# A macaron layer on eight sequences: feed-forward blocks swapped, k projected inside the recurrence, gram products ahead of v, first block unbroken ahead of the mixture, all FIR behind it

## The reference, cut to what matters

```
x = x + 0.5 * ffn(layernorm(x))            # ffn: 256 -> 1024, gelu, 1024 -> 256
x = x + attn(layernorm(x))
x = x + 0.5 * ffn(layernorm(x))            # the same weights

def attn(x):                               # 4 heads of 64
    q, k, v = silu(short_conv(x @ Wq)), ... Wk, ... Wv          # causal, 4 taps
    beta = sigmoid(x @ Wb)                                      # one number a token and head
    delta = delta_rule(l2norm(q), l2norm(k), v * beta, k * beta) # chunks of 32: triangular inverse,
                                                                 # then a recurrence over chunks
    branches = [fir(v, 3 taps), fir(v, 31 taps), delta, v]
    w = softmax(gate(x, mean/rms/max of each branch, branches) / temp), floored, normalised
    o = rmsnorm(sum of w * branch)
    return o @ Wo
```

## Time and profile before

| | us |
|---|---|
| runs | 1223.7, 1226.2, median 1224.95 |
| the profiled execution | 1227.37 |
| its span in the trace | 1225.7 |
| TensorE busy | 1056.4 (86%) |
| VectorE busy | 820.9 (67%) |
| ScalarE busy | 549.3 (45%) |
| GpSimd busy | 415.6 (34%) |
| start of y1 (L883) of the seven passes with a back half and of the tail | 144.32, 287.65, 422.66, 558.97, 694.00, 833.65, 969.01, 1100.62 |

### The profile page before, as it was taken

How to read it: one execution, slowest core, us unless ns; L and a number is a source line. 1 busy time by engine, 2 the same in 40 slices (tenths; PEclk the granted TensorE clock), 3 DMA queues, 4 the chain that set the end, 5 groups by cost and what they waited for, 6 DMA issues and landing times.

```text
span 1225.7 us, 25639 instructions
## 1 busy us (share of the span) xinstructions
PE 1056.4 (86%) x10348; PEld 784.7 (64%) x10348; DVE 820.9 (67%) x1556; ACT 549.3 (45%) x965; POOL 415.6 (34%) x648
## 2 busy tenths in 40 slices
PE   3778598899988999899988996999988998887838
PEld 2654485378745886488736884478736885477427
DVE  5774267785687767875788666875787667863263
ACT  1154236443374337543475336453475337532322
POOL 7106500671019500681028400681028400870000
PEclk9889699899999999989999999999999999995668
DMA  5040104110040203111040203011040204020000
GB/s 153 1 102 21 34 1 97 25 31 22 18 104 1 53 1 94 28 26 27 19 104 1 52 19 86 18 24 30 18 104 1 52 1 96 9 52 1 1 0 18
DMA packets 82293, 47.45 MB, mean 39 GB/s; under 512 B 57856, under 2 KB 75776, under 8 KB 82176
## 3 DMA queue, kind: packets, MB, share of 16 engines
q1 hardware_dynamic: 82176, 45.82, 16.4%
HBM read 31.12 MB, written 14.68 MB: 37 GB/s over the span
## 4 chain that ended last, share of the span: by engine, by line
PE 57%; DVE 22%; ACT 8%; issue 5%; SPq 3%; POOL 3%; DMA 1%; DVEq 0%; ACTq 0%; POOLq 0%
PE psum L782 12%; PE psum L784 10%; PE psum L783 10%; DVE conv_acc L1363 4%; PE psum L813 4%; DVE arena L1594 3%; PE psum L975 3%; PE psum L960 3%; PE psum L994 2%; PE psum L999 2%; SPq L347 2%; PE psum L1152 2%; ACT arena L582 2%; DVE arena L1596 2%; POOL arena L522 1%
## 5 line engine op out<-in xcount | busy, mean ns | idle before, releaser
L518 POOL TENSOR_TENSOR l_prod<-arena 64x30 f32<-64x30 f32 (+14 forms) x240 | 150.8, 628 | 599.2 <-DMA arena<-l_dram 581.0
L578 ACT ACTIVATE h_f<-psum,b_col 128x512 f32<-128x512 f32 x128 | 88.0, 688 | 216.4 <-PE psum L784 206.4
L522 POOL TENSOR_TENSOR arena<-arena,l_prod 64x30 f32<-64x30 f32 (+14 forms) x240 | 157.3, 655 | 18.8
L782 PE MATMUL psum<-w_hi,h_hi 128*128 128x256 f32 x512 | 152.0, 297 | 9.2 <-DVE h_lo L1343 9.2
L784 PE MATMUL psum<-w_hi,h_lo 128*128 128x256 f32 x512 | 145.2, 284 | 0.0
L783 PE MATMUL psum<-w_lo,h_hi 128*128 128x256 f32 x512 | 145.1, 283 | 0.0
L1081 PE MATMUL psum<-v_shift,fir_w 128*32 128x512 f32 x1152 | 133.6, 604 | 3.6 <-DMA v_shift<-v_dram 3.6
L1363 DVE SCALAR_TENSOR_TENSOR conv_acc<-psum,conv_col,conv_acc 128x511 f32<-128x511 f32 x144 | 107.8, 748 | 33.5 <-ACT conv_acc L603 22.4
L782 PE MATMUL psum<-xt_hi,w_hi 128*128 128x512 f32 x256 | 109.4, 427 | 14.3 <-DVE b_half L1456 7.0
L1342 DVE CAST h_hi<-h_f 128x512 fp32r<-128x512 f32 x128 | 65.3, 510 | 76.6 <-ACT h_f L578 40.1
L782 PEld LDWEIGHTS psum<-w_hi,h_hi 128*128 128x128 f32 x512 | 98.1, 192 | 15.3 <-DVE h_lo L1343 11.1
(11 more groups left out here) (232 smaller groups left out, 2205.6 us busy)
## 6 DMA issues: line engine op xcount, KB each, us to landing
x_in<-in_L_attn_x SPq DMA_DIRECT2D x8, 512.0 KB, 4.0
v_dram<-v_fm SPq DMA_DIRECT2D x8, 512.0 KB, 2.8
v_shift<-v_dram SPq DMA_DIRECT2D x8, 512.0 KB, 5.0
out<-x_tok SPq DMA_DIRECT2D x8, 512.0 KB, 2.9
v_shift<-v_dram SPq DMA_DIRECT2D x8, 511.0 KB, 7.0
v_shift<-v_dram SPq DMA_DIRECT2D x8, 510.0 KB, 9.1
v_shift<-v_dram SPq DMA_DIRECT2D x8, 509.0 KB, 11.6
arena<-in_L_ffn_w SPq DMA_DIRECT2D x2, 1024.0 KB, 7.1
```

What stands on the lines that cost most here:

```text
L518: pool.tensor_tensor(prod, l_inv[:, k + 1:, k:k + 1].broadcast_to(shape), l_inv[:, k:k + 1, 0:k].broadcast_to(shape), ALU.mult).then_inc(i ...
L522: pool.tensor_tensor(l_inv[:, k + 1:, 0:k], l_inv[:, k + 1:, 0:k], prod, ALU.add).then_inc(inverted, 1)
L578: act.activation(h_f[:, m % 2, :], bank, ACT.Gelu, bias=b1_col[:, m:m + 1]).then_inc(read, 1)
L782: pe.matmul(dst, a_hi, b_hi, start=first, stop=False, **kw)
```

## The change

- The blocks change places. The filler of the merge and the recurrence is now the **second** block of sequence i - 1 (`upr`, `outr`); the **first** block of sequence j + 1 (`upw`, `outw`) stands as one piece behind `hidden` and ahead of the FIR. The program is now head, "zero" (a body without filler), five bodies, last, tail. Head holds two blocks (of sequences 0 and 1), zero one, each body two, last one, tail two: 16 as before.
- The second layer norm's turn goes into the end of the recurrence (tiles 2 and 3), k's first half is projected in tile 3, where `gate_f` 0 and 1 stood, its second half right behind.
- beta: 24 matmuls with the tokens as weights and 4 moving columns give it in token layout at once; before, 6 matmuls, a copy through Sigmoid and 4 turns.
- k's turn and gram products stand ahead of `gate_d` and v; l_tok goes to DRAM ahead of v.
- All 144 FIR matmuls stand behind the first block: 88, then `mix_t`, 24, then `Wo`, 32.
- The three copies of a sequence's rows (x_in, x1_tok, x2_tok) become a ring of three tiles in place, and GpSimd's copy from x1 to x2 is gone; the bias adds remain. Sequence 1 is loaded at setup, y stored at the start of the next pass.
- On VectorE, statistics, `normalise` and the low half of the next sequence's first layer norm move into the middle of the pass, between `k_rows` and the clamp and among the `hidden` adds; the splits of the first block stand among convolutions, softmax and mixture.

The core of the diff (TensorE's stream of a pass, then VectorE's; ScalarE follows in the same manner):

```
-                else:
-                    gate_f(at, 0)
-                    gate_f(at, 1)
+                elif at.front:
+                    copied(pe, at, "ln2", 0)
+                    copied(pe, at, "ln2", 1)
+                    projection(at, "k", 0, 0)
...
+                if at.front:
+                    projection(at, "k", 1, 0)
+                if at.back:
+                    gate_f(at, 0)
+                    gate_f(at, 1)
+                if at.front:
+                    beta(at)
                 if at.back:
                     gate_f(at, 2)
                     gate_f(at, 3)
...
                 if at.front:
-                    turn_rows(at, "ln2", xn_made[1], j + 1)
+                    pe.wait_ge(silu_made, 6 * j + 2)
+                    to_tok(at, "k_t", lambda h: qk_fm[:, h, 0, :])
+                    k_products(at)
...
+                if at.ahead:
+                    turn_rows(at, "ln1", xn_made[0], j + 2)
+                    wide(range(0, 8))
                 if at.back:
                     bank, full = claim(pe, at, "logit")
...
+                if at.ahead:
+                    wide(range(8, 12))
                 if at.back:
                     copied(pe, at, "logit")
                     turn(at, "logit_t", 0, lambda t: lg_fm[:, P * t:P * t + P])
-                if at.front:
-                    firs(at, 0, range(1, 9))
+                if at.ahead:
+                    wide(range(12, 16))
+                if at.front:
                     pe.wait_ge(silu_made, 6 * j + 6)
                     to_tok(at, "q_t", lambda h: qk_fm[:, h, 1, :])
-                    firs(at, 1, range(0, 8))
...
+                if at.ahead:
+                    wide(range(28, 32))
+                if at.front:
+                    pe.wait_ge(v_shifted, 64 * j + 64)
+                    firs(at, 0, range(0, 9))
+                    firs(at, 1, range(0, 2))
                 if at.back:
                     for b in range(2):
                         pe.wait_ge(norm_made, 2 * i + b + 1)
                         turn_tiles(at, "mix_t", b)
...
+                if at.front:
+                    k_rows()
+                if at.ahead:
+                    x_ready(dve, j + 1)
+                    stats(0, rows_of(j + 1))
+                if at.front:
+                    conv(2)
+                if at.ahead:
+                    normalise(0, j + 1, rows_of(j + 1))
                 if at.back:
                     copied(dve, at, "stat")
                     link(dve.tensor_scalar(stat_fm[0:D, :], stat_fm[0:D, :], 1e-4, None, ALU.max))
                     dve.sem_inc(stat_made, 1)
...
                 if at.front:
                     conv(4)
+                    wide_split(0)
                     conv(5)
+                    wide_split(1)
...
                         link(dve.tensor_tensor(src[:, :, :, :], src[:, :, :, :],
                                                mix_w[:, :, s:s + 2].unsqueeze(3).broadcast_to([P, UNITS, 2, D]), ALU.mult))
+                        if at.front:
+                            wide_split(3 + n_src)
```

More of the change, by code:

```diff
@@ L191, in macaron_kernel @@
-        both = [MERGE, RECUR, FFN_A, STATS, LN2, V, STAT, K, LOGIT, FIR, Q, MIX, V_T, FFN_C, L_OFF]
-        ORDER = {"head": sum(front + [NEXT], first), "body": sum(both + [NEXT], []),
-                 "last": sum(both, []), "tail": sum(back, [])}
+        FFN_R = [("upr", (2, 3) + (2,) * (KT - 2)), ("outr", (3, 4))]
+        LN2 = [("ln2", (2, 7))]
+        K = [("k", (2, 7)), ("beta", (0,))]
+        GATE = [("gate", (5, 6, 3, 4)), ("dv_t", (1, 0, 1, 0))]
+        GRAM = [("k_t", (2, 7)), ("gram", (0, 1))]
@@ L540, in one_pass @@
                     pool.wait_ge(t_zeroed, 2 * j + 2)
-                if at.back:
-                    pool.wait_ge(xn_made[2], 2 * at.i + 2)
-                    for t in range(TILES):
-                        last = pool.tensor_tensor(x2_tok[:, t, :], x2_tok[:, t, :], b2_half[:, :], ALU.add)
-                    last.then_inc(bias2_added, 1)
-                    pool.wait_ge(bias2_added, at.i + 1)
+                if not at.front:
+                    add_bias(at.i, 2, bias2_added)
             every_pass(pool, one_pass)
@@ L691, in one_pass @@
-                    if not at.back:
-                        act.wait_ge(c_loaded, C_LOADED * 16)
-                    tap(0)
+                    out_of(at, "beta", 0, rows_tok[:, 1, :].rearrange("p (t h) -> p t h", t=TILES), ACT.Sigmoid,
+                           src=lambda b: b[:, 0:TILES * 32].rearrange("p (t h) -> p t h", t=TILES)[:, :, 0:HEADS])
+                if at.back:
+                    for h in range(2):
+                        out_of(at, "dv_t", h, dv_fm[h])
+                if at.front:
+                    silu(0)
+                    silu(1)
@@ L716, in one_pass, with wide_gelu @@
                 if at.front:
-                    tap(5)
+                    out_of(at, "hidden", 0, hid_fm[:, :])
+                def wide_gelu(m):
+                    if at.wide:
+                        gelu(at, 1, at.w, m)
+                if at.front:
+                    wide_gelu(0)
+                    wide_gelu(1)
                 if at.back:
@@ L1187, in one_pass @@
                     off_diagonal(at, "lhalf")
-                attend_at, pair_at, next_at = 16, 20, len(STEPS) - 4
-                if at.back:
+                    attend(at, 0)
+                if at.keep:
+                    turn_rows(at, "next", xn_made[2], 2 * i + 2)
+                if at.front:
+                    attend(at, 1)
+                    off_diagonal(at, "lpair")
+                if not at.front:
                     for b in range(2):
```

532 lines of the change are left out of this document (279 added, 253 removed).

## The result

The changed kernel took **1291.05 us** (1290.1 and 1292.0) against 1224.95: 1.054 times the kernel before, 95% interval 1.048 to 1.060. In a second series it was 1.0536 (1.0495 to 1.0577). So it is slower, as forecast, by 66 us where the forecast had 41, and 1 us above the range of 1201 to 1290.

| pass | before | forecast | after |
|---|---|---|---|
| head | 144.3 | 150.1 | 152.35 |
| zero | 143.3 | 150.9 | 149.7 |
| five bodies (in all) | 681.4 | 727.5 | 740.5 |
| last | 131.6 | 116.7 | 125.3 |
| tail | 125.1 | 121.1 | 122.2 |

What follows compares the result with a forecast made beforehand. TensorE was taken to bound a body, with VectorE pacing it in the first block. Passes of 150.1 + 150.9 + 5 x 145.5 + 116.7 + 121.1 gave 1266.3, plus 1.7, less 2.4 to the median: 1266 us, range 1201 to 1290.

Steps and rivals of the forecast that it cites:

- the walk: One body followed in each engine's new order with durations of before, clock 0 at y1: 145.5 us against 136.3.
- k's turn: TensorE gets there at 48.6 and waits 2.1 us for ScalarE's silus, until 50.7.
- `gate_stats`: TensorE, done at 61.8, waits 3.9 us for VectorE's clamp at 65.7, then returns at the lower clock.
- The 3.0: Extra us at `gate_stats` and the projection behind it for the lower clock, taken from the tail's `gate_stats`.
- First block: 76.0 to 110.3, paced by VectorE; waits of 1.1 for the low half, 2.0 for a gelu, 5.5 for splits.
- Behind it: After the first block: 28.4 us of FIR, `mix_t`, `Wo`, turns and small products, plus 2.5 for `lpair`, to 141.2.
- the 145.5: Forecast length of one body in us: 141.2 plus 4.25 for the filler's six steps ahead of y1.
- the six: TensorE's waits for splits, `gate_stats`' clamp, `lpair`, k's silu, the third up product's gelu and the first's low half.
- the **last** pass: A body minus the first block (22.8) and 12.5 of waits, plus 6.5 for the mixture: 116.7 us.
- The head's terms: Head before, plus a block, minus 11.0 of waiting for the inverses and 2.8 for v_shift: given as 150.1 us.
- C: Rival: VectorE does not pace the first block, its waits go, 15 us in six passes, 1176 us; chance 0.12.
- D: Rival: beside GpSimd's inversion eight splits cost 1.0 us more each, 8 us in six passes, 1314 us; chance 0.05.

Runs made afterwards that it cites:

- the four edits: Changed kernel with k's silus first, mixture behind the splits (`mix_t`, `Wo` later), clamp first, `lpair`'s wait behind the filler: 0.991 times the kernel before.

## Why the prediction was right about the way, and which steps of its sum failed

The way and the mechanism were right: each wait came where the walk had it. One body against the walk, with 598.69 as its zero:

- *k's turn.* Start forecast at 50.7 with a wait of 2.1; measured 51.9, with 1.8. TensorE came 1.5 late, since the matmuls ahead of it ran at half clock. This was not in the sum:

```profile
643.21 2.56 PE L1044 MATMUL psum<-f_fm,gate_w 128*128 128x512 f32 x4
645.56 3.26 PE L855 MATMUL psum<-ident,arena 128*128 128x128 f32 x16
650.63 1.40 PE L855 MATMUL psum<-ident,qk_fm 128*128 128x128 f32 x8 [1.80 <-ACT qk_fm L621]
```

 In the one body where the granted clock held at 1.00 up to there (451.53), TensorE came at 48.8, where the walk had 48.6.
- *`gate_stats`.* Forecast ready at 65.7, wait 3.9, clock low behind it. Measured:

```profile
665.41 1.14 PE L1059 MATMUL psum<-stat_fm,gate_st 32*128 32x512 f32 x8 [2.28 <-DVEq L1636]
666.81 1.14 PE L1059 MATMUL psum<-stat_fm,gate_st 32*128 32x512 f32 x8 [0.26 <-PE psum L1059]
```

 Start at 66.7, wait 2.3 as TensorE came later itself, and the full clock: each half took 1.14 as in the earlier trace rows, not the 2.2 taken from the tail's row. The 3.0 did not come in this body. In three of the five the clock did fall here, in two it held. One of each, from `gate_stats` to the first block, first where it fell (wait 2.84), then where it held (wait 3.14):

```profile
960.10:969.22 9.12, 7.72 (x36) 4.54 (x37) 4.46 (x7) 2.97 (x6) 7.95 (x18) 0.81 0.35 113
813.11:820.64 7.53, 6.13 (x36) 3.79 (x37) 4.46 (x7) 2.85 (x5) 6.59 (x16) 1.00 0.25 78
```

 The fall costs 1.6 us; spread over the five bodies that is 1.0 each, a third of the 3.0.
- *First block.* Forecast 76.0 to 110.3, with 1.1, 2.0 and 5.5 of waits; measured 74.3 to 111.1, with 1.1, 1.5 and 6.8. VectorE's operations were dearer than taken: a split 1.61 against 1.38 to 1.42 (1.43 in the earlier trace rows), the mixture's four 9.5 against 8.2. In the earlier trace rows, also beside the inversion, its two products stood back to back and took 4.62; here each stands between splits and takes 2.64. The granted clock of this stretch was 0.96 in four bodies of five.
- *Behind it.* The filler was to start 30.9 later, with a wait of 2.5 for `lpair`; measured 30.8 (740.55) and 2.3. Its six steps then took 5.7 instead of 4.25, at a clock of 0.75. In one body of five the same wait of 2.30 was followed by the full clock, and they took 4.4:

```profile
740.55:746.23 5.68, 5.68 (x19) 4.29 (x19) 1.65 (x4) 2.70 (x4) 0.00 (x0) 0.75 0.00 0
888.21:892.57 4.36, 4.36 (x18) 3.28 (x19) 1.65 (x4) 2.70 (x4) 0.00 (x0) 1.00 0.01 4
```

So the first step that failed is the term for the clock. I put 3.0 us of it at one place, where it was worth 1.0, and none at others where it fell in most bodies: around k's turn, in the first block, and behind `lpair`. The sum over the five bodies says the same. A body came to 148.1 in the mean, 2.6 above the 145.5, 13 us in five. The waits were not what was missing: the six came to 16.1 a body where the sum had 17.1. TensorE's busy time was 131.1 where the sum left at most 128.4 for it; the same matmuls take 126.5 in the kernel with the four edits, at a clock of 0.99.

The second step that failed is the **last** pass: 125.3 against 116.7, the other 9 us. I had subtracted the first block and its waits from a body, and so overlooked what the block covered. Its waits:

```profile
PE psum L1125 <- DMA v_shift<-v_dram: 4.4, 1, 4.4
PE psum L855 <- ACT qk_fm L621: 3.5, 2, 1.8
PE psum L824 <- DVE v_shift L1616: 2.9, 1, 2.9
```

The FIR waits 4.4 for v's shifted copies, the turns of k and q wait for their silus, and most of the filler's first steps run at half clock; the mixture, for which I had put 6.5, costs 1.6. Head (+2.2), zero (-1.2) and tail (+1.1) were near. The head's terms (144.3 + 22.8 - 11.0 - 2.8) add up to 153.3 and not to the 150.1 that went into the sum; that is nearer to what was measured, and the forecast would have been 1269. A block of 96 times 0.235 is 22.6, not 22.8, which changes little. Of the rivals, C (VectorE does not pace the first block) is refuted by the h_lo waits, and D (GpSimd's hold on VectorE) is real but smaller than its price: 0.49 us a split and not 1.0, and the sum held a part of it already.

What remains open: why the clock falls behind one wait and not behind another. The length of the wait alone does not tell: at `lpair` 2.30 was followed by either level, and at `gate_stats` it held behind 3.14 and fell behind 2.84. Beta's narrow matmuls are not the cause behind `gate_f`; no run separates the rest.

## What to carry to other kernels

When work is moved next to other work of the engine that feeds the bound engine, walk both in-order streams through the new stretch with durations of the trace: sums over the pass showed VectorE with 36 us to spare, and yet small waits at a few places cost 5%. What stood between a producer's operation and the one that the consumer waited for was paid as a wait, and often once more through the clock; so put the released operation first (clamp, silu, split) and the bulk behind it, and ask what the next wait takes back. And when a block is taken out of a stretch, ask what it had covered.

## What was not expected of the hardware

- A split and a product of the mixture were slower by 0.49 and 0.36 us beside GpSimd's inversion, while a convolution row, which reads one operand from PSUM, took 0.75 with and without it. Leaving the inversion's work out was worth 2.5% of the time, though GpSimd is never on TensorE's list of waits.
- 24 matmuls with 4 moving columns went at 0.11 us each, about as those of 128 columns did at the full clock (8 in 1.09); replacing them by 6 wide ones and 4 turns gained nothing.
- Without the waits, TensorE's busy time in five bodies fell from 655.6 to 632.7 us for the same instructions, and the granted clock rose from 0.96 to 0.99: some 23 us of these bodies went with the clock.
- The same wait at the same place of the program was followed by the full clock in one body and by half of it in another.
